# Two attention layers over 32 images: a new order of work in the slots and in the fill

## The reference

```
layer 0:  h = group_norm(x, 32 groups) * w + b
          q, k, v = qkv_w @ h + qkv_b
          a = softmax(q^T k / sqrt(128))            1024 x 1024 for each image
          x1 = x + proj_w @ (v a^T) + proj_b
layer 1:  q, k = Wq @ x1 + bq, Wk @ x1 + bk         16 channels each
          v = Wv @ x1 + bv
          a = softmax(q^T k)                        no scale
          out = gamma * (v a^T) + x1
```

## Time and profile before

| what | before |
| --- | --- |
| median of 3 runs | 1596.41 us |
| profiled execution, its span | 1597.02 us, 1594.9 us |
| PE busy, weight loads busy | 1509.8 us (95%), 1094.5 us (69%) |
| DVE busy | 1297.1 us (81%) |
| ACT busy | 1205.2 us (76%) |
| POOL busy | 1237.1 us (78%) |
| granted TensorE clock, mean | 0.993 of full |
| idle of ACT before L465, waiting for L565 | 295.2 us in 256 waits |
| idle of DVE before L582, waiting for L473 | 136.7 us in 255 waits |

### The profile page before, as it was taken

How to read it: one execution, slowest core, us unless ns; L and a number is a source line. 1 busy time by engine, 2 the same in 40 slices (tenths; PEclk the granted TensorE clock), 3 DMA queues, 4 the chain that set the end, 5 groups by cost and what they waited for, 6 DMA issues and landing times.

```text
span 1594.9 us, 43924 instructions
## 1 busy us (share of the span) xinstructions
PE 1509.8 (95%) x16777; PEld 1094.5 (69%) x16777; DVE 1297.1 (81%) x2508; ACT 1205.2 (76%) x1698; POOL 1237.1 (78%) x1027
## 2 busy tenths in 40 slices
PE   5899999999999999999999999999999999999987
PEld 2466777767777767777767777767767767777766
DVE  5678888888888888888888888888888888888875
ACT  2577777777778777778777778777778777778774
POOL 3688888888788888788888788888788888788653
PEclk9899999999999999999999999999999999999999
DMA  3699999999999999999999999999999999999999
GB/s 78 120 161 192 192 202 199 191 202 201 208 191 199 202 200 200 193 201 198 204 194 198 205 191 202 197 205 199 198 195 195 207 192 206 199 192 189 190 187 179
DMA packets 1081438, 305.22 MB, mean 191 GB/s; under 512 B 1068272, under 2 KB 1068944, under 8 KB 1081232
## 3 DMA queue, kind: packets, MB, share of 16 engines
q1 hardware_dynamic: 1080080, 302.41, 108.4%
q10 hardware_dynamic: 1152, 0.00, 0.0%
HBM read 17.13 MB, written 16.78 MB: 21 GB/s over the span
## 4 chain that ended last, share of the span: by engine, by line
PE 47%; ACT 23%; DVE 15%; issue 11%; POOL 2%; SPq 1%; DMA 1%; ACTq 0%; DVEq 0%; POOLq 0%
DVE nmax L565 10%; ACT prob L460 10%; ACT scores L465 9%; PE mixed L816 7%; PE mixed L818 7%; PE mixed L817 7%; PE scores L771 6%; PE scores L772 4%; PE scores L773 4%; PE scores L801 3%; PE bank_w L890 3%; PE bank_t L836 2%; PE bank_w L882 2%; ACT v_head L517 2%; DVE qk L635 2%
## 5 line engine op out<-in xcount | busy, mean ns | idle before, releaser
L816 PE MATMUL mixed<-v_head,pt 128*128 128x129 f16 x4096 | 713.3, 221 | 1.9 <-DMA pt<-rows 1.9
L818 PE MATMUL mixed<-v_head,pt 128*128 128x129 f16 x4096 | 713.1, 219 | 0.0
L817 PE MATMUL mixed<-v_tail,pt 128*128 128x128 f16 x4096 | 713.1, 218 | 0.0
L565 DVE TENSOR_REDUCE nmax<-scores 128x1 f32<-128x1024 f32 x512 | 601.5, 1216 | 46.1 <-PE scores L801 28.5
L366 POOL TENSOR_TENSOR rows<-prob,rows 128x1024 f16<-128x1024 f32 x256 | 545.2, 2130 | 21.4
L465 ACT ACTIVATE scores<-scores,nmax 128x1024 f32<-128x1024 f32 x256 | 278.6, 1088 | 295.2 <-DVE nmax L565 295.2
L361 POOL TENSOR_SCALAR rows<-prob 128x1024 f16<-128x1024 f32 x256 | 267.0, 1043 | 268.0 <-ACT prob L460 265.8
L582 DVE SCALAR_TENSOR_TENSOR rows<-scores,rows 128x1024 f16<-128x1024 f32 x256 | 313.5, 1225 | 136.7 <-ACT rows L473 136.7
L817 PEld LDWEIGHTS mixed<-v_tail,pt 128*128 128x128 f16 x4096 | 403.8, 99 | 2.7
L816 PEld LDWEIGHTS mixed<-v_head,pt 128*128 128x128 f16 x4096 | 397.0, 97 | 2.6 <-DMA pt<-rows 2.2
L818 PEld LDWEIGHTS mixed<-v_head,pt 128*128 128x128 f16 x4096 | 395.0, 96 | 0.0
(11 more groups left out here) (110 smaller groups left out, 1849.0 us busy)
## 6 DMA issues: line engine op xcount, KB each, us to landing
x_raw<-in_x_dram SPq DMA_DIRECT2D x32, 512.0 KB, 4.9
out_dram<-y SPq DMA_DIRECT2D x64, 256.0 KB, 3.0
pt<-rows SPq DMA_TRANSPOSE x512, 4.9
w_qkv<-in_L_conv_qkv_w_dram SPq DMA_DIRECT2D x3, 64.0 KB, 4.1
b_qk<-in_L_conv_bk_dram SPq DMA_DIRECT2D x8, 0.1 KB, 2.3
b_qk<-in_L_conv_bq_dram SPq DMA_DIRECT2D x8, 0.1 KB, 1.9
w_proj<-in_L_conv_proj_w_dram SPq DMA_DIRECT2D x1, 64.0 KB, 4.8
w_v<-in_L_conv_Wv_dram SPq DMA_DIRECT2D x1, 64.0 KB, 4.7
```

The lines of the kernel that those rows point to most:

```text
L565: nc.vector.reduce_max(nmax[l][:, tile.i % TILES:tile.i % TILES + 1], scores[l][:, :], AX.X, negate=True).then_inc(maxed[l], 1)
L816: mm(mixed[l][:, 0:C + 1], head, vh[:, p, m, 0:C + 1], start=(m == 0), stop=False)
L817: mm(mixed[l][:, 0:C], head, vt[:, p, m, :], start=False, stop=False)
L818: done = mm(mixed[l][:, 0:C + 1], tail, vh[:, p, m, 0:C + 1], start=False, stop=(m == TILES - 1))
```

## The change

Six things change, all of them in the order or the slot of work. The instructions themselves and their number stay the same.

1. PE makes the scores of layer 1 ahead of those of layer 0, where before the layer-1 tile stood between the two halves of the layer-0 tile.
2. DVE makes the tails of the projections of slot s in slot s+1, between the two row maxima; before it made them in slot s, behind `invert`.
3. ACT does the two norms of a slot ahead of the evictions of that slot's projections, and copies QK1 behind the exponentials and not ahead of them.
4. V of layer 0 is projected in positions 0 and 1 and not 1 and 2.
5. In the fill: the second half of image 2's statistics one slot earlier, the fourth QK projection of image 0 one slot later, V of image 0 in slots 1 and 2 (before -1 and 0), the folding of the projection's weights later (PE ahead of slot 0, DVE ahead of slot 1, before both ahead of -2), the setting up for QK1 one slot later, `X_BIAS` of image 0 in slot 2 (before 0), V1 of image 0 in slots 10 and 11 (before 8 and 11).
6. PE's `evicted_here` is left out in slots that have no tile to turn back.

```diff
--- before.py
+++ after.py
@@ -39,7 +39,7 @@
 SWING, ATTEND, ADD = (1, 0), 3, 4
 FIRST_SLOT = -16
 
-SETUP_QK, SETUP_V, SETUP_FOLD, SETUP_QK1, SET_UP = -8, -5, -2, 1, 3
+SETUP_QK, SETUP_V, SETUP_FOLD, SETUP_QK1, SET_UP = -8, -5, (0, 1), 2, 3
 BIASED = -6
 
 
@@ -113,21 +113,21 @@
 
 LOADS = Steps(-16)
 LOADS_LEFT = -11
-STATS = Steps(-12, -11, first={1: (-11, -11), 2: (-9, -8)})
+STATS = Steps(-12, -11, first={1: (-11, -11), 2: (-9, -9)})
 GN = Steps(-10, -9, first={2: (-8, -7)})
 ROOT, H_FULL = Steps(-8, first={1: (-9,), 2: (-6,)}), Steps(-7, first={1: (-8,), 2: (-5,)})
 H_HEAD, H_TAIL = Steps(-7, first={2: (-5,)}), Steps(-6, first={1: (-7,), 2: (-4,)})
-X_BIAS = Steps(-5, first={0: (0,), 1: (1,), 2: (0,), 3: (-4,)})
-QK = Steps(-5, -4, -3, 0, first={0: (-5, -4, -3, -2), 1: (-4, -3, -2, -1), 2: (-4, -3, -2, 0)})
-QK_SPLIT = Steps(-4, -3, -2, 1, first={0: (-5, -4, -3, -2), 1: (-3, -2, -1, 0), 2: (-3, -2, -1, 1)})
+X_BIAS = Steps(-5, first={0: (2,), 1: (1,), 2: (0,), 3: (-4,)})
+QK = Steps(-5, -4, -3, 0, first={0: (-5, -4, -3, -1), 1: (-4, -3, -2, -1), 2: (-4, -3, -2, 0)})
+QK_SPLIT = Steps(-4, -3, -2, 1, first={0: (-5, -4, -3, -1), 1: (-3, -2, -1, 0), 2: (-3, -2, -1, 1)})
 H_TAIL_FIRST = -6
-V_SLOTS = {0: (-1, 0), 1: (-1, 0)}
+V_SLOTS = {0: (1, 2), 1: (-1, 0)}
 QK1_SLOTS = {0: (6, 7), 1: (8, 11), IMAGES - 1: (10, 11)}
-V1_SLOTS = {0: (8, 11), 1: (9, 10), IMAGES - 1: (13, 14)}
+V1_SLOTS = {0: (10, 11), 1: (9, 10), IMAGES - 1: (13, 14)}
 
 V, QK1, V1 = (0, 1), (2, 3), (4, 5)
-W = Steps(1, 2, 11, 15, 12, 14,
-          first={n: V_SLOTS.get(n, (1, 2)) + QK1_SLOTS.get(n, (11, 15)) + V1_SLOTS.get(n, (12, 14))
+W = Steps(0, 1, 11, 15, 12, 14,
+          first={n: V_SLOTS.get(n, (0, 1)) + QK1_SLOTS.get(n, (11, 15)) + V1_SLOTS.get(n, (12, 14))
                  for n in (0, 1, IMAGES - 1)})
 QK1_COPY = Steps(12, 16, first={n: tuple(slot + 1 for slot in QK1_SLOTS[n]) for n in QK1_SLOTS})
 X1_BIAS = Steps(15, first={0: (9,), IMAGES - 1: (12,)})
@@ -519,13 +519,16 @@
                                      ACT.Copy).then_inc(v1_headed, 1)
 
             def body(slot):
-                for im, h in QK1_COPY.at(slot):
-                    qk1_copy(im, h)
                 if tile := TILE_AT[1].get(slot):
                     exponent1(tile)
                     head_row1(tile)
                 if tile := TILE_AT[0].get(slot):
                     exponent0(tile)
+                for im, h in QK1_COPY.at(slot):
+                    qk1_copy(im, h)
+                for lane in range(2):
+                    if tile := TILE_AT[lane].get(slot - ATTEND):
+                        norm(tile)
                 for im, part in W.at(slot):
                     if part in V:
                         v_head_out(im, part - V[0])
@@ -537,9 +540,6 @@
                     qk_copy_out(im, j)
                 for im, _ in H_HEAD.at(slot):
                     h_head_out(im)
-                for lane in range(2):
-                    if tile := TILE_AT[lane].get(slot - ATTEND):
-                        norm(tile)
 
             act.dma_start(gnw[:, :], col(gn_w)).then_inc(gn_loaded, 16)
             act.dma_start(gnb[:, :], col(gn_b)).then_inc(gn_loaded, 16)
@@ -723,6 +723,13 @@
             def body(slot):
                 if tile := TILE_AT[1].get(slot):
                     row_max(tile)
+                for im, part in W.at(slot - 1):
+                    if part in V:
+                        v_tail_out(im, part - V[0])
+                    elif part in QK1:
+                        qk1_tail_out(im, part - QK1[0])
+                    else:
+                        v1_tail_out(im, part - V1[0])
                 if tile := TILE_AT[0].get(slot):
                     row_max(tile)
                     exp_bias(tile)
@@ -736,13 +743,6 @@
                 for lane in TILE_AT:
                     if tile := lane.get(slot - ATTEND):
                         invert(tile)
-                for im, part in W.at(slot):
-                    if part in V:
-                        v_tail_out(im, part - V[0])
-                    elif part in QK1:
-                        qk1_tail_out(im, part - QK1[0])
-                    else:
-                        v1_tail_out(im, part - V1[0])
                 for im, h in STATS.at(slot):
                     gn_first(im, h)
                 if slot == H_TAIL_FIRST:
@@ -757,9 +757,9 @@
             setup_qk()
             every_slot(body, SETUP_QK, SETUP_V)
             setup_v()
-            every_slot(body, SETUP_V, SETUP_FOLD)
+            every_slot(body, SETUP_V, SETUP_FOLD[1])
             setup_fold()
-            every_slot(body, SETUP_FOLD, SETUP_QK1)
+            every_slot(body, SETUP_FOLD[1], SETUP_QK1)
             setup_qk1()
             every_slot(body, SETUP_QK1)
 
@@ -944,27 +944,24 @@
                 for im, step in GN.at(slot):
                     gn_product(im, step)
                 first, second = (lane.get(slot + 1) for lane in TILE_AT)
-                if first and first.layer == 0:
-                    score0(first, 0)
-                elif first:
-                    score1(first)
-                if second and second.layer == 1:
-                    score1(second)
-                elif second:
-                    score0(second, 0)
-                    score0(second, 1)
-                if first and first.layer == 0:
-                    score0(first, 1)
-                evicted_here(slot)
+                for tile in (second, first):
+                    if tile and tile.layer == 1:
+                        score1(tile)
+                for tile in (second, first):
+                    if tile and tile.layer == 0:
+                        score0(tile, 0)
+                        score0(tile, 1)
+                if any(here):
+                    evicted_here(slot)
                 for tile in here:
                     if tile:
                         back(tile)
 
             every_slot(body, FIRST_SLOT, SETUP_QK)
             setup_turns()
-            every_slot(body, SETUP_QK, SETUP_FOLD)
+            every_slot(body, SETUP_QK, SETUP_FOLD[0])
             setup_fold()
-            every_slot(body, SETUP_FOLD, SET_UP)
+            every_slot(body, SETUP_FOLD[0], SET_UP)
             pe.wait_ge(setup_dve, DVE_ALL)
             every_slot(body, SET_UP)
```

## The result

The changed kernel takes 1584.8 us (median of 8 runs, 1577.4 to 1592.3), the kernel before 1596.9 (8 runs, 1596.1 to 1598.1). The ratio is 0.9922, 95% interval 0.9907 to 0.9938: 0.8% faster, 12 us. The forecast was 1555 us, in a range of 1522 to 1582; the time lies above both. The runs of the changed kernel also lie 15 us apart where those of before lie 2 us apart.

A forecast was written before the change was run, and what follows sets the result against it. Each slot was taken to last the longer of PE's work and a wait loop through DVE, ACT and PE. Gains of 33 + 3.5 + 1.5 + 3.5 = 41.5 us gave 1555 us, range 1522 to 1582.

The forecast's parts named there:

- The steady term of the sum: Slots 16 to 240: 28 images, each 1.19 us shorter than 47.87, gain 33 us.
- New loop of 5.21 us: Steady slots: the wait loop through DVE, ACT and PE, from one L801 to the next, takes 5.21 us.
- Undisturbed image 46.68: Steady part: the eight positions of an image sum to 46.68 us, 1.19 less than 47.87.
- Fill, slot 3 at 55 to 56 and 3.5 us gained: Fill: slot 0 starts 4 us sooner, but transposes queue behind a load; slot 3 starts 3.5 us earlier than 59.3.
- Slots 3 to 16, 1.5 us: After the fill: slots bound by PE's 48 matmuls, little changes, 1.5 us gained.
- The end, 3.5 us: The 16 slots from 240 on, without QK: the short loop shows, 3.5 us less than 90.7.
- The norms' wait for L577, 0.3 us a slot: ACT: the norms, now ahead of evictions, get a wait for L577 of some 0.3 us in each slot.
- A: Steady part: PE keeps its own pace, all waits filled, 45.4 us an image, 1520 us in total; chance 0.14.
- B: Steady part: DVE's rounds bind as late work delays the next maximum, 47.3 us an image, total 1573; chance 0.22.
- C: Steady part: late QK evictions make PE's `back` and next `attend` wait on `bank_t`; slower, 1616 us; chance 0.06.
- D: Whole kernel: waits only move, the tails' 1.2 us an image are not hidden, 1589 to 1597 us; chance 0.08.
- The sign set beforehand: Steady part: an image's period above 47.3 or below 46.0 us makes the forecast wrong.

The follow-up runs named there:

- e6: Changed kernel with three row buffers a lane, image 3's load three slots later, and loads and stores issued by ACT's queue: 1569.1 us.
- e9: Kernel of e5 with loads (from image 3 on) and all stores carrying only 2 columns, result incomplete: 1533.4 us.
- e8: Kernel of e7 plus item 1 alone, PE's layer-1 scores ahead of layer 0's: 1596.4 us.
- e10: Kernel before with only items 5 and 6 of the change, the fill: 1596.0 us, ratio 0.9993.
- e4: Changed kernel with half of every transpose, heads only, the head read again for the tail, result incomplete: 1539.6 us.
- e7: Kernel before with half of every transpose, heads only, result incomplete: 1596.7 us, ratio 0.9993.
- e5: Changed kernel with three row buffers a lane instead of two and image 3's load three slots later: 1579.9 us.

## Why the prediction was wrong

The step that failed is this: "A slot then lasts as long as the longer of this loop and PE's work, since both run from L801 to L801." The list of what a slot can wait for had two members and needed a third, the transposes' way through SP and the DMA engines. They were priced in the fill only, where a load stood in front of them. The steady term of the sum, 33 us, measured 1.9; that is the miss.

What the profile of before had on it: the DMA share of 1.13 at 199 GB/s in the earlier trace rows, which has no place in the argument. By the transposes' own row of before

```profile
L304 SPq DMA_TRANSPOSE pt<-rows x512: 1316/2398/4114, 34.1 to 1583.6; - x171
```

the median is 2.40 us, and the mean from slot 16 to 240, each read by itself, 2.55. With some 0.18 between two, 16 of them are 43.7 us, and a load and two stores with their own 0.18 add 2.8: 46.5 of 47.87 were taken. That sum says 46.68 is just possible, and it is wrong too, because a transpose's time isn't a constant: the mean grew to 2.62 in the changed kernel and 2.76 in e6. What hardly moved is the rate. An image moves 199 x 47.87 = 9.5 MB. To take 46.24 us in the mean it needs 206 GB/s, and the most that any run with the whole data sustained over 800 us is 201. (Single images took 46.2 us all the same; the buffers let the transposes fall behind for a while.) Against that 201, before, at 199, had 1% of room for a change that was to bring 2.5%. That the ceiling lies at 201 is read from these runs alone, and no row of before tells it; that the DMA share stands above 1 there is what should have made a rival of it. The share alone doesn't decide it either: e9, which nothing in the transfers holds up, still shows 1.11.

The Trainium skill has both halves of this. "DMA: Bandwidth & Descriptors", section on issuing engines not being separate DMA queues, says that DMAs run on the same 16 engines whoever issues them, and that a second issuer saves only sequencer time. The runs agree: 10.8 us by issuing elsewhere, 46.5 by moving less. "Perfetto Trace Analysis", section on what "DMA-bound" means, says that where the issuing sequencer's track is solid DMA slices the bound is the sequencer, and the window is the generation of descriptors and not the moving of data. Here the measurement decides against it: SP's track is solid in the changed kernel, yet the same transpose takes 1.32 to 4.96 us there, and with other transfers' data taken away and no instruction fewer the time falls by 46.5 us.

Point by point:

- **New loop of 5.21 us:** right, 5.21 in e8.
- **Undisturbed image 46.68:** 46.24. Positions 1 and 2 take 11.00 (11.21), positions 5 to 7 16.75 (16.96): late starts that I added are partly hidden. The 5.41 for position 5 in that step is not the 5.32 of the list of eight, and no row is given for it; the list's own 5.32 + 5.78 + 5.75 = 16.85 comes nearer. The mechanism of PE, ACT and DVE was right.
- **33 us over 28 images:** 1.9. Failed, as above. With half the transposes it is 28 x (47.87 - 46.25) = 45 us.
- **Where the 1.56 us between 46.25 and 47.81 go:** 44 us over 28 images. 27.3 us at half clock do the work of 13.7, so up to 13.7 of the 44 are clock, the rest the waits themselves.
- **Fill, slot 3 at 55 to 56 and 3.5 us gained:** 55.7 and 3.6; slot 0 started 5.0 us sooner (4), slots 0 and 1 lasted 7.8 and 8.4 (8.3, 8.9), the transposes started at 42.85 behind the load. Right in size and cause, and ACT's row head waited 6.37 us for it:

```profile
49.23 1.02 ACT L473 ACTIVATE rows<-scores 128x1024 f16<-128x1024 f32 x1 [6.37 <-DMA pt<-rows]
55.69 1.09 ACT L465 ACTIVATE scores<-scores,nmax 128x1024 f32<-128x1024 f32 x1 [3.36 <-DVE nmax L565]
```

- **Slots 3 to 16, 1.5 us:** 83.4 before, 80.7 after, 2.6. But e10 shows that the fill by itself gives that back; what stays comes with the order.
- **The end, 3.5 us:** 90.7 before, 89.2 after, 1.5. With half the transposes 87.3, so 3.3: the same third member again.
- **The norms' wait for L577, 0.3 us a slot:** 88.2 us in 203 times, 0.43 each, somewhat more than forecast; the undisturbed image is still shorter than forecast.
- **Rivals:** A (45.4) is out, since e4 and e9 stay at 46.25 without the transposes' limit. B (47.3) is out for the same reason. C is out by the wait for L488. D's 1589 came nearest to the time, for the wrong reason: in the undisturbed image the tails are hidden.
- **The sign set beforehand,** a period above 47.3 makes the forecast wrong, was met: 47.81.

The terms close: 1.9 (steady) + 3.6 + 2.6 (to slot 16) + 1.5 (slots 240 to 256) + 0.2 (behind them) = 9.8 us, and the spans differ by 1594.9 - 1585.0 = 9.9; the rest is rounding. What stays open: which part of the movement is full, the DMA engines themselves or something on their way to and from the buffers. No run parts these. Nor is it known whether the loads and stores cost so much by their bytes as such or because they go to and from the tensors in DRAM; e4 shows only that transposes' bytes count too.

## What to carry to other kernels

When a change shortens the loop of the compute engines, list every other stream that runs once a slot, DMA queues too, and ask at what period each is full; here two limits stood some 0.1 us an image apart, removing the first gave 12 us, removing the second alone (e7) nothing, and both 57. A queue's busy time is a poor measure of that: look whether the rate (GB/s) stays put while the load changes, and try it by taking away the data and not the instructions. And moves that look separate may not pay one by one: order and tails gave next to nothing until the copies and norms had moved too.

## What the runs showed of the hardware

- **A DMA transpose has no fixed price on its queue.** The same 512 KB instruction took 1.32 to 4.96 us in the changed kernel, mean 2.62 between slots 16 and 240, and half of it took 1.23 at the median. Landing took 5.1 us at the median after its issue, 3.1 for the half and 4.9 with thin loads and stores.
- **Small waits can cost clock.** In a wait of PE of 3.21 us, in a stretch in which it was otherwise busy, the granted clock fell for 6.8 us. Between slots 16 and 240 the time at the lower level is 27.3 us in the changed kernel, 13.7 in e5, 6.8 in e6, none before, in e4 or in e9. Not every such wait was followed by a fall.
- **Issuing elsewhere frees little when the movement is full.** SP gave away 2.3 us of loads and stores an image in e6, and its transposes took 2.0 us more.
- **The changed kernel's runs scatter, and the limit of transfers alone does not account for it.** They lie within 15 us in the changed kernel, 2 before, 1.0 in e4 and 1.0 in e9; but within 2.7 in e5, which is as bound by its transfers, and 5.2 in e7, which is not. The cause was not looked for.
